# Row maxima from 64-row products of the high parts, two query tiles side by side in TensorE's rows

## The reference

```python
qkv = jnp.einsum('bte,fe->btf', x, Wqkv).reshape(B, T, H, 3 * D)      # H = 8, D = 64, T = 2048
q, k, v = jnp.split(qkv, 3, axis=-1)
q = q + pe[None, None]
k = k + pe[None, None]
scores = jnp.einsum('bhtd,bhsd->bhts', q, k) / jnp.sqrt(D)
scores = jnp.where(causal, scores, -jnp.inf)
probs = jax.nn.softmax(scores, axis=-1)
attn = jnp.einsum('bhts,bhsd->bhtd', probs, v)
out = jnp.einsum('btf,ef->bte', out, Wo)
```

## Time and profile before

| | |
|---|---|
| median of 3 runs | 699.99 us (699.36 to 701.64) |
| profiled execution | 701.03 us, of which the span of the trace is 699.3 us |
| granted TensorE clock, mean | 0.969 of full speed |
| TensorE busy (PE) | 646.9 us, 93% of the span |
| GpSimd busy (POOL) | 500.3 us, 72% |
| VectorE busy (DVE) | 497.7 us, 71% |
| ScalarE busy (ACT) | 448.8 us, 64% |

### The profile page before, as it was taken

How to read it: one execution, slowest core, us unless ns; L and a number is a source line. 1 busy time by engine, 2 the same in 40 slices (tenths; PEclk the granted TensorE clock), 3 DMA queues, 4 the chain that set the end, 5 groups by cost and what they waited for, 6 DMA issues and landing times. The chain is left out here.

```text
span 699.3 us, 10129 instructions
## 1 busy us (share of the span) xinstructions
PE 646.9 (93%) x3215; PEld 494.5 (71%) x3215; DVE 497.7 (71%) x1048; ACT 448.8 (64%) x626; POOL 500.3 (72%) x289
## 2 busy tenths in 40 slices
PE   4889999999999999999999999999797899989883
PEld 4557777777777777877777777776586687667661
DVE  3577678777876866867877786682287878776684
ACT  3437676677676766667677667676456477657561
POOL 7007888888987888889888798889753347567660
PEclk9989999999999999999999999999988899999996
DMA  7432322222212321232122322106000000000001
GB/s 195 99 83 62 75 47 47 52 69 62 47 45 58 79 48 45 47 85 53 45 47 59 78 47 46 46 1 176 22 2 1 0 1 1 1 15 1 15 0 30
DMA packets 27460, 33.75 MB, mean 48 GB/s; under 512 B 6897, under 2 KB 13842, under 8 KB 27282
## 3 DMA queue, kind: packets, MB, share of 16 engines
q1 hardware_dynamic: 27410, 33.14, 19.8%
HBM read 6.84 MB, written 1.05 MB: 11 GB/s over the span
## 5 line engine op out<-in xcount | busy, mean ns | idle before, releaser
L333 POOL TENSOR_TENSOR probs_l<-probs,probs_h 128x1024 fp32r<-128x1024 f32 (+1 forms) x160 | 347.4, 2185 | 103.4 <-ACT probs_h L373 57.3
L427 DVE TENSOR_REDUCE m_part<-max_ps 128x1 f32<-128x512 f32 (+2 forms) x320 | 180.0, 601 | 86.2 <-PE max_ps L503 65.1
L370 ACT ACTIVATE probs<-scores 128x1024 f32<-128x1024 f32 (+1 forms) x160 | 150.5, 940 | 126.9 <-PE scores L531 67.4
L563 PE MATMUL out_ps<-probs_h,v 128*128 128x512 f32 (+5 forms) x640 | 186.1, 374 | 2.1 <-POOL probs_l L333 2.1
L373 ACT ACTIVATE probs_h<-scores 128x1024 fp32r<-128x1024 f32 (+1 forms) x160 | 149.7, 936 | 0.0
L530 PE MATMUL scores<-q,k 128*128 128x512 f32 (+1 forms) x320 | 122.7, 384 | 0.0
L832 POOL TENSOR_TENSOR hid_lo<-hid,hid_hi 128x512 fp32r<-128x512 f32 x64 | 84.0, 1317 | 53.8 <-ACT hid_hi L912 41.1
L531 PE MATMUL scores<-q,k 128*128 128x512 f32 (+1 forms) x320 | 116.8, 365 | 0.0
L563 PE MATMUL out_ps<-probs_l,v 128*128 128x512 f32 (+1 forms) x320 | 116.4, 364 | 0.0
L563 PEld LDWEIGHTS out_ps<-probs_h,v 128*128 128x128 f32 (+1 forms) x640 | 95.7, 163 | 23.9 <-POOL probs_l L333 5.8
L503 PE MATMUL max_ps<-k,q 128*128 128x512 f32 (+2 forms) x320 | 103.2, 398 | 6.2 <-DVE m_part L427 5.9
(11 more groups left out here) (195 smaller groups left out, 979.8 us busy)
## 6 DMA issues: line engine op xcount, KB each, us to landing
k<-qk SPq DMA_DIRECT2D x96, 128.0 KB, 2.3
q<-qk SPq DMA_DIRECT2D x96, 128.0 KB, 2.3
q<-m_turn SPq DMA_DIRECT2D x128, 0.5 KB
v_all<-L_ffn_ew SPq DMA_DIRECT2D x2, 768.0 KB, 8.1
pos<-positions SPq DMA_DIRECT2D x1, 1024.0 KB, 6.8
out<-v_all SPq DMA_DIRECT2D x4, 256.0 KB, 2.3
acc<-L_attn_Wqkv SPq DMA_DIRECT2D x2, 256.0 KB, 4.0
v_all<-L_attn_Wo SPq DMA_DIRECT2D x2, 256.0 KB, 6.5
```

The costliest lines, as they stand in the source:

```text
L333: pool.tensor_tensor(probs_l[:, p % 2, :, lo:CH], probs[:, p % 2, :, lo:CH], probs_h[:, n % 3, :, lo:CH], ALU.subtract).then_inc(S["probs_ ...
L370: act.activation(probs[:, p % 2, :, lo:CH], scores[:, p % 2, :, lo:CH], ACT.Exp, scale=D ** -0.5).then_inc(S["probs_ready"], 1)
L427: dve.tensor_reduce(m_part[:, r, j:j + 1], max_ps[:, u % 2, 0:width], AX.X, ALU.max).then_inc(S["tile_max_ready"], 1)
L563: last = pe.matmul(o_ps(h, c)[0:rows, lo:CH], v, pr, start=(p == PAIR0[c] and j == 0 and k == 0), stop=(p == PAIR0[c + 1] - 1 and j == 1 a ...
```

## The change

1. **The product of a unit.** `maximum` reads 64 rows instead of 128, the half given by `half_rows(r)`: partitions 0 to 63 for even tiles, 64 to 127 for odd ones. It is high times high alone. Each such matmul has a TensorE tile of 64 rows by 128 columns, at row 0 or row 64, where it was 128 by 128.
2. **The places of q's parts.** For odd tiles, the low part lies in partitions 0 to 63 of `q1` and the high part in 64 to 127. `tiles_of` picks the even or odd tiles of a chunk, and each of the two moves into `q1` becomes two, so there are eight moves for a chunk in place of six. `k1` is the same in both halves, so the scores' matmul with `q1` gives the same sum as before.
3. **Which signal counts what.** The two moves of the high part count for `max_operands_moved`. The moves of the low part now count for `score_operands_moved`, which the maximum units don't wait for.
4. **The order of units.** Within two tiles the units go (tile r, keys j), (tile r + 1, keys j), then the next j: the two units of a slot are the two halves, with the same keys.
5. **The masks.** `mask_maximum` issues the mask products of both units after both products, instead of each after its own.

```diff
 def unit_place(u):
     c = chunk_of(UNIT0, u)
-    r, j = divmod(u - UNIT0[c], c + 1)
+    two, half = divmod(u - UNIT0[c], 2)
+    rows, j = divmod(two, c + 1)
+    r = 2 * rows + half
     return c, r, j, (CH if j < c else P * (r + 1))
+
+
+def half_rows(r):
+
+    return slice(r % 2 * D, (r % 2 + 1) * D)
+
+
+def tiles_of(ap, s):
+
+    return ap.rearrange("d (g s j) -> d g s j", s=2, j=P)[:, :, s, :]
...
-                        move(q1[0:D, qs], qk_hi[0:D, :], "max_operands_moved")
+                        for s in range(2):
+                            move(tiles_of(q1[half_rows(s), qs], s), tiles_of(qk_hi[0:D, :], s), "max_operands_moved")
                         sp.wait_ge(S["qk_low_ready"], of * NC + c + 1)
-                        move(q1[D:P, qs], qk_lo[0:D, :], "max_operands_moved")
+                        for s in range(2):
+                            move(tiles_of(q1[half_rows(1 - s), qs], s), tiles_of(qk_lo[0:D, :], s), "score_operands_moved")
                         move(q2[0:D, qs], qk_hi[0:D, :], "score_operands_moved")
                         move(k2[0:D, of % 2, ks], qk_lo[D:P, :], "score_operands_moved")
...
-                        wait(act, S["score_operands_moved"], 32 * n)
+                        wait(act, S["score_operands_moved"], 64 * n)
...
-                last = pe.matmul(max_ps[:, u % 2, 0:n], q1[:, tile:tile + P], k1[:, h % 2, ks], start=True, stop=(j < c))
+                last = pe.matmul(max_ps[:, u % 2, 0:n], q1[half_rows(r), tile:tile + P], k1[half_rows(r), h % 2, ks], start=True, stop=(j < c))
+                if j < c:
+                    last.then_inc(S["max_scores_ready"], 1)
+
+            def mask_maximum(h, u):
+                c, r, j, width = unit_place(u)
                 if j == c:
-                    last = pe.matmul(max_ps[:, u % 2, width - P:width], mask_kq[:, P:2 * P], ident_b[:], start=False, stop=True)
-                last.then_inc(S["max_scores_ready"], 1)
+                    pe.matmul(max_ps[:, u % 2, width - P:width], mask_kq[:, P:2 * P], ident_b[:],
+                              start=False, stop=True).then_inc(S["max_scores_ready"], 1)
...
                     for of, u in units(p, h):
                         maximum(of, u)
+                    for of, u in units(p, h):
+                        mask_maximum(of, u)
```

More of the change, by code:

```diff
@@ L294, in _ @@
             sp.wait_ge(S["max_operands_moved"], 64 * H * NC)
-            sp.wait_ge(S["score_operands_moved"], 32 * H * NC)
+            sp.wait_ge(S["score_operands_moved"], 64 * H * NC)
             sp.wait_ge(S["v_low_ready"], 2 * H)
@@ L410, in section @@
                         wait(dve, S["max_operands_moved"], 64 * n)
-                        wait(dve, S["score_operands_moved"], 32 * n)
+                        wait(dve, S["score_operands_moved"], 64 * n)
                         dve.tensor_tensor(qk_lo, projected_ps(of, c), qk_hi, ALU.subtract).then_inc(S["qk_low_ready"], 1)
@@ L518, in score_pair @@
                     pe.wait_ge(S["max_row_moved"], 64 * (h * NC + c + 1))
-                    pe.wait_ge(S["score_operands_moved"], 32 * (h * NC + c + 1))
+                    pe.wait_ge(S["score_operands_moved"], 64 * (h * NC + c + 1))
                 wait(pe, S["probs_high_ready"], h * NP + p - 1)
```

## The result

The changed kernel takes 726.25 us (724.91 to 727.04, 4 runs), the kernel before 700.82 us in the same measurements (699.36 to 703.14, 4 runs). The recorded ratio is 1.0336, 95% interval 1.0313 to 1.0359. The two medians alone lie 25.4 us apart, a ratio of 1.036, so the change costs 3.4 to 3.6%. The forecast was 676 us, within 661 to 700.

A forecast was written before the change was run, and what follows sets the result against it. TensorE was taken to bound the attention. Savings of 31.7 + 3.2 - 5 = 30 us, less 6 kept by other engines, gave 24 us off the 699.99 median: 676 us, whole range 661 to 700.

The forecast's parts named there:

- What bounds the kernel: In the attention, TensorE sets the pace: busy in all 57.21 us of a head, with GpSimd at 48.39 and VectorE 43.01.
- Two units side by side: In each pair of unit products, both halves stream together and cost the wider member: 31.7 us saved.
- Switching between 128-row and 64-row products: Twice a slot, 320 times, around the pair: taken as 0, with an upper bound of 0.25 us a switch, 80 us.
- the rival: Each row-shape switch around the pair empties the array, up to 80 us against 30 saved: 750 us, 705 to 750; chance 0.18.
- Weight loads of the pair: Both loads must hide behind the product ahead of the pair: 0.03 us a pair, 5 us lost, between 0 and 14.
- rival 1: Products overlap, but visible half-row loads (14 us) or VectorE and GpSimd (up to 20 us) take most gain: 690 us; chance 0.14.
- Moves: Two more DMAs a chunk in SyncE's queue, 1.3 us a chunk: costed at nothing, 41 us if the cover were gone.
- Masks behind both: Of 128 unit masks, 64 are followed by the other mask, not a stalled product: 3.2 us saved, between 0 and 5.8.
- VectorE keeps a part: In slots 2 to 5, VectorE has only 0.38 us to spare, so about 0.4 us a head of TensorE's saving is lost.
- the part of GpSimd's chain: In slots 12 to 19, waiting on the chain through GpSimd loses another 0.4 us a head of TensorE's saving.

The follow-up runs named there:

- full rows: The changed kernel with every unit's product back at 128 rows, the maximum units waiting for all eight moves: 708.29 us, ratio 1.0096.
- units apart: The changed kernel with a slot's second unit issued behind the PV products, each unit's mask right behind it: 828.94 us, ratio 1.1804.

## Why the prediction was wrong

The profiled executions of all runs split at the first and the last score product. The start is counted from the first addition of the positions, since the loads ahead of it vary by 2 us. Times in us:

| run | start to first scores | first to last scores |
|---|---|---|
| before | 27.6 | 450.6 |
| order of units | 28.9 | 452.2 |
| order, masks behind both | 28.8 | 451.6 |
| eight moves only | 30.3 | 450.7 |
| order, masks, eight moves (full rows) | 32.4 | 452.0 |
| changed kernel | 34.1 | 469.4 |
| changed, 64 rows off the diagonal only | 33.1 | 462.1 |
| changed, both units in the lower half | 37.7 | 497.7 |
| score masks behind both blocks | 27.3 | 447.0 |
| first score moves on GpSimd | 27.8 | 450.5 |
| both of these | 27.9 | 447.1 |

The kernel before and the runs with eight moves only and with moves on GpSimd run the same products in the heads, and so do the two with score masks. They agree to 0.2 us (450.5 to 450.7, and 447.0 and 447.1), so the second column can be trusted to a few tenths.

From before to the changed kernel this is 6.5 us in the start and 18.8 us in the heads. The stretch behind the last scores is 1.5 us shorter (202.0 to 200.5), which means nothing: it lies between 200.5 and 204.8 in the profiles of all these kernels, which don't differ there. Together it is the 23.9 us of the spans, with 0.1 before the start.

**What bounds the kernel: right.** PE is busy through the attention before and after, and the time follows what it is given.

**Two units side by side: right.** 31.7 us forecast, 34.7 measured between the two runs that differ only in the half of the array that the second unit uses (in the profiles 28.3 in the heads and 3.6 in the start, 31.9 together).

**Switching between 128-row and 64-row products: this is the step that failed.** I wrote: "So a change of the column shape costs nothing, and I take 0 for the row shape." The row on which this rested was right for what it showed, but it was a row about another shape. For rows the price is about 0.2 us a change: 0.39 for the two changes of a slot by the rows, 0.21 each by units apart. In the changed kernel it is 0.09 + 0.19 + 0.11 = 0.39 in a slot whose pair has no mask beside it, and less beside some masks. In a head, 16 slots enter at 0.09 and 4, behind a score mask of 128 columns, at 0.03. 12 leave at 0.30 and 8, on the diagonal, at 0.20. That is 1.6 + 3.6 + 1.6 = 6.8 us, 54 us in all. Less the 31.7 saved it is 22 us, and less some 4 us in which the run with full rows waits for VectorE inside its pairs (see below) and the changed kernel hardly does, 18 us. From full rows to the changed kernel the table measures 17.4 in the heads. I had the rival with its place, its point of decision (0.09 us a change) and its upper bound (0.25), and gave it 0.18. The range ended at 700 because of that. The price is not the same on both sides, though, as that rival had it: 0.09 on the way in and 0.30 on the way out. How it forms was only read, not tested alone. By the PEld rows the load at each change starts with its own product and not behind the one ahead, and the product seems to begin when the one ahead has left the array. The 0.11 behind the pair is about the 0.09 behind a mask.

**Weight loads of the pair: too small.** I put 0.03 us a pair, because two loads of 0.13 would not fit behind one product. Measured is 0.09 ahead of the pair, the 14 us in all that rival 1 named for a half-row load that can't be hidden. It isn't the sum of two loads, since a single unit pays the same 0.09 (units apart). I had priced this and the change of shape as two things; on the way in they are one, and the runs can't part them.

The Trainium skill's rule that was weighed in the prediction ("TensorEngine Tiling (Array Packing)", section Tiling Modes: changing the mode drains TensorE) agrees with the trace for rows, 0.21 us a change. It does not agree for columns, where the earlier trace rows have a 128-by-64 product between two full ones with no loss.

**Moves: wrong in the start.** "I cost it at nothing" holds in the heads (450.7 against 450.6). In the start, two moves more a chunk delay the first scores by 2.7 us, and the buffer `qk` is what couples them: ScalarE's copy of the next chunk waits until all moves out of it have landed. I looked at SyncE's own waits over the whole span and not at the stretch in which nothing else hides the queue.

**Masks behind both, and the order of units.** I counted 3.2 us of gain for the masks and nothing for the order. The order costs 1.6 us in the heads and 1.3 in the start, and the masks give back 0.6 of the former. The forecast that VectorE keeps a part was right in its place (PE waits for `m_part` in slots 4 to 6), as far as the run with full rows can show it. Its size for a faster TensorE, like the part of GpSimd's chain, could not be seen, since TensorE got slower. In the run with full rows, slots 5 and 6 of the head show PE waiting inside the pair:

```profile
118.97 0.80 PE L518 MATMUL max_ps<-k,q 128*128 128x512 f32 x2
119.61 0.39 PE L583 MATMUL out_ps<-probs_h,v 128*128 128x256 f32 x2
...
121.30 0.84 PE L518 MATMUL max_ps<-k,q 128*128 128x256 f32 x2
121.98 0.28 PE L525 MATMUL max_ps<-ident_b,mask_kq 128*128 128x128 bf16 x2
```

The first pair takes 0.64 us instead of 0.46. The second, two units of 256 behind a mask, takes 0.68 where its columns and one stall ask for 0.24 + 0.09. With 0.05 in slot 4 that is 0.6 us a head. That grouping masks does gain where VectorE isn't behind it is shown by the score masks: 3.6 us in the heads (3.4 when both kernels have their first moves on GpSimd), with 3.2 forecast by the same sum.

**What stays open.** In the start the changed kernel is 1.7 us later than the run with full rows (in which the units even wait for all eight moves), and three causes lie together there: the changes of shape, the longer idle times, and a lower granted clock. PE sat idle for 3.04 us up to 29.10 (1.45 us up to 27.66 in the kernel before), and over the whole start the mean granted clock was 0.77 of 2.4 GHz (the lower level is 1.2), against 0.82 in the run with full rows and 0.90 before (the changed kernel's first product after the gap, its start, and the start of the kernel before; the clock is the third number from the end):

```profile
29.10 1.12 PE L517 MATMUL max_ps<-k,q 64*128 64x384 f32 x2 [3.04 <-DVE m_part L441]
...
19.20:53.30 34.10, 25.60 (x81) 14.55 (x79) 17.86 (x35) 11.44 (x20) 0.00 (x0) 0.77 0.35 81
```

```profile
19.10:46.70 27.60, 21.59 (x82) 14.16 (x81) 17.91 (x35) 11.51 (x20) 0.00 (x0) 0.90 0.46 106
```

## What to carry to other kernels

Two half-row products in different halves of the array do run at the same time, but each change between half-row and full-row products costs about 0.2 us, nearly as much as the 0.23 us that a pair of 512 columns saves. So one pair a slot doesn't pay. By these prices several pairs together between two changes would: two pairs would save 0.46 us against 0.39. That is an estimate from the numbers above, and no run here tests it. A neighbour with the same cost is no proof for an operation that differs in another dimension. Where only such a row exists, the forecast should lean on the point from which the rival decides (here 0.09 us), and keep the other side in the range. And a queue that is slack over the whole program may set the pace in its start, so a moved or added DMA is to be costed in each stretch by itself.

## What the runs showed of the hardware

- A change from 128-by-128 to 64-by-128 products and back: 0.39 us in a slot without masks (0.09 on the way in, 0.30 on the way out), and at most 0.21 us a change between two runs that differ by 320 changes. A change from 128-by-128 to 128-by-64 and back: nothing.
- At a change of row shape the next weight load starts with its own product, where between two full-row products of 512 columns it starts 0.23 us ahead, while the one before still runs. At a change of column shape it starts ahead as well.
- Two half-row products in different halves take as long as one (0.42 us for two of 512 columns, and 0.42 for one alone). In the same half they follow one another (0.66 us for two), 34.7 us more for 160 pairs.
- Two bf16 masks of 128 columns in a row take 0.10 us together, so the second one's load shows by about 0.02, not by the 0.09 of a full float32 product behind a mask.
- With six moves of one chunk issued by SyncE and GpSimd at the same time, SyncE's moves of `q` took 3.3 us from issue to landing, and GpSimd's 2.7 and 3.4. Issued one after the other by SyncE alone, they took 2.3.
